# Splitting the expert matrices inside the last attention batch

## The reference

```python
x = x + attention(layernorm(x))          # 16 heads of 32, window of 128 and 4 sink columns
x = x + experts(layernorm(x), token_ids) # below
x = x + ffn(layernorm(x))                # 8-bit activations, ternary weights, hidden 2048
...
tid = clip(token_ids, 0, VOCAB - 1)
expert_ids = minimum(tid // (VOCAB // 4), 3)
for e in range(4):                       # Wg = Wu = Wd = ctx, 4 x 512 x 512
    g = silu(h @ Wg[e].T); u = h @ Wu[e].T
    y = (g * u) @ Wd[e].T
    out = where(expert_ids == e, y, out)
```

## Time and profile before

| | us |
|---|---|
| median of 3 runs | 949.4 (948.38 to 952.41) |
| the profiled execution | 942.91 |
| its span, first to last instruction | 941.4 |
| TensorE busy, whole span | 839.4 (89%) |
| VectorE, ScalarE, GpSimd busy | 628.5, 517.8, 265.0 |
| attention ends, experts begin | about 560.6 |
| experts end, last stage begins | about 713 |

### The profile page before, as it was taken

The page is one execution under the profiler, slowest core; times in us unless marked ns, Lnnn a source line. Parts: engine busy times, 40 slices in busy tenths (PEclk is TensorE's granted clock), DMA queues, the critical chain, the costliest instruction groups (busy, mean ns, idle before and its releaser), DMA issues. The chain is left out here.

```text
span 941.4 us, 17497 instructions
## 1 busy us (share of the span) xinstructions
PE 839.4 (89%) x6031; PEld 545.4 (58%) x6054; DVE 628.5 (67%) x1122; ACT 517.8 (55%) x1136; POOL 265.0 (28%) x258
## 2 busy tenths in 40 slices
PE   4897999979999979999998864999993899999996
PEld 3664666656666756666765543888871344444443
DVE  6655754646655446656456637788863999999994
ACT  4254665545665435666466622544432777777775
POOL 1061301110310011211013124454422444444442
PEclk9998999999999979999999996999997999999998
DMA  7345421462442173344083018446202011110100
GB/s 246 69 106 142 112 72 51 105 143 105 113 113 64 50 180 101 79 113 113 23 234 81 2 53 324 155 152 218 93 37 89 3 44 45 45 45 33 34 34 34
DMA packets 36740, 90.68 MB, mean 96 GB/s; under 512 B 6846, under 2 KB 6846, under 8 KB 35008
## 3 DMA queue, kind: packets, MB, share of 16 engines
q1 hardware_dynamic: 31216, 73.97, 28.0%
q0 software_dynamic: 5456, 15.74, 4.9%
HBM read 52.71 MB, written 13.39 MB: 70 GB/s over the span
## 5 line engine op out<-in xcount | busy, mean ns | idle before, releaser
L457 ACT ACTIVATE probs<-s_ps,neg_max 128x512 f32<-128x512 f32 (+2 forms) x256 | 153.4, 607 | 35.7 <-DVE neg_max L606 34.7
L464 ACT ACTIVATE probsT<-pT_ps 128x512 f32<-128x512 f32 (+1 forms) x128 | 76.2, 596 | 140.1 <-PE pT_ps L815 139.5
L815 PE MATMUL pT_ps<-ident,probs 128*128 128x128 f32 (+1 forms) x960 | 148.0, 283 | 2.5 <-ACT probsT L464 2.5
L606 DVE TENSOR_REDUCE neg_max<-s_ps 128x2 f32<-128x1024 f32 (+2 forms) x128 | 130.6, 1021 | 24.8 <-PE s_ps L796 21.3
L626 DVE COPY probsT<-pT_ps 128x512 f32<-128x512 f32 x112 | 77.4, 691 | 85.5 <-PE pT_ps L815 85.0
L815 PEld LDWEIGHTS pT_ps<-ident,probs 128*128 128x128 f32 (+1 forms) x960 | 101.4, 135 | 35.3 <-issue 23.7
L831 PE MATMUL pv_ps<-probsT,v_sb 128*32 128x128 f32 (+1 forms) x1920 | 102.7, 286 | 11.0 <-DVE probsT L626 9.0
L789 PE MATMUL s_ps<-qk_stack 96*128 96x512 f32 (+2 forms) x256 | 94.8, 438 | 16.0 <-issue 12.1
L1372 POOL TENSOR_TENSOR hw<-h,ln_w_sb 128x512 f32<-128x512 f32 x64 | 81.8, 1278 | 90.3 <-DVE h L1487 90.2
L831 PEld LDWEIGHTS pv_ps<-probsT,v_sb 128*32 128x32 f32 (+1 forms) x1920 | 37.8, 107 | 82.1 <-issue 55.4
L367 POOL TENSOR_TENSOR rinv_wide<-rinv,one_col 128x512 f32<-128x512 f32 x16 | 16.7, 1043 | 227.0 <-DVE rinv L613 227.0
(11 more groups left out here) (236 smaller groups left out, 1804.6 us busy)
## 6 DMA issues: line engine op xcount, KB each, us to landing
qk_stack<-qk_parts SPq DMA_DIRECT2D x192, 128.0 KB, 2.5
w_piece<-w_ffn SPq DMA_DIRECT2D x24, 512.0 KB, 3.7
w_stage<-w_ffn SPq DMA_DIRECT2D x12, 1024.0 KB, 5.1
xres<-x POOLq DMA_DIRECT2D x4, 1024.0 KB, 6.3
xt<-x SPq DMA_DIRECT2D x16, 256.0 KB, 2.6
y<-xt SPq DMA_DIRECT2D x16, 256.0 KB, 2.0
xn<-x SPq DMA_DIRECT2D x3, 1024.0 KB, 11.1
x<-xres POOLq DMA_DIRECT2D x3, 1024.0 KB, 7.7
```

Of the source, the lines that this page charges most:

```text
L457: nc.scalar.activation(probs[:, qt % 2, h, 0:width(qt)], s_ps[:, h, 0:width(qt)], ACT.Exp, bias=neg_max[:, qt % 2, h:h + 1], accum_out=sum ...
L464: nc.scalar.activation(probsT[0:rows, 0, :], pT_ps[0:rows, 0, :], ACT.Identity).then_inc(slot_copied[0], 1)
L606: nc.vector.tensor_reduce(neg_max[:, qt % 2, 2 * s:2 * s + 2], s_ps[:, 2 * s:2 * s + 2, 0:width(qt)], AX.X, ALU.max, negate=True).then_inc ...
L815: last = nc.tensor.transpose(pT_ps[0:z - a, k % 2, h * P:h * P + P], probs[:, qt % 2, h, a:z], ident[:])
```

## The change

- `w_hi` and `w_lo` of the attention become one shared buffer of four places, and the experts' `c_hi` and `c_lo` are the same buffer. Expert `e` overwrites the place of the matrix number `e` of q, k, v, o.
- Experts 0 to 2 are split in the last batch, at the ends of units (2, 0), (2, 2) and (3, 1): `expert_hi` on ScalarE behind the unit's exponentials, `expert_lo` on VectorE behind the unit's last copy. SyncE loads experts 2 and 3 into `xn` and `v_next` when the subtractions of experts 0 and 1 are done. The place of `o` is in use to the end of attention, so expert 3 is split in the expert stage (`last_hi`, `last_lo`).
- `w_piece` is shared, and GpSimd clears it at the end of attention. It holds tiles 0 and 1; `xg_own` has 9 tiles and is cleared at once. The first gather waits for nothing, the second for nothing but the constants before it, the third for the clear.
- On VectorE the last expert's subtraction stands behind `xT_lo` of tile 0; TensorE waits for it ahead of the first product and for no expert after.
- SyncE waits for the second gather instead of the first, and then issues weight chunks only. The last stage's `xt` is `xn`.

```diff
...
 RING = 4
-OWN_TILES = ROUTED_TILES - 2 * TT
+FIRST_TILES = 2
+OWN_TILES = ROUTED_TILES - 2 * TT - FIRST_TILES
 GATHERS_AHEAD = 6
-CLEARED_AT_ONCE = 2
-CLEARS = 3
 ROUTE_COUNTED, ROUTE_STEPS = 10, 32
...
         xn, v_next = sh["xn"], sh["v_next"]
 
-        w_hi = {n: sb(f"w{n}_hi", [P, DK, D], F32R) for n in "qkvo"}
-        w_lo = {n: sb(f"w{n}_lo", [P, DK, D], F32R) for n in "qkvo"}
+        w_hi = {n: sh["w_hi"][:, i * DK:i * DK + DK, :] for i, n in enumerate("qkvo")}
+        w_lo = {n: sh["w_lo"][:, i * DK:i * DK + DK, :] for i, n in enumerate("qkvo")}
...
 
         abs_sum = sh["abs_sum"]
-        w_piece = sb("w_piece", [P, CHUNK // 2])
...
         rstd_ready, xn_ready = sem("rstd_ready"), sem("xn_ready")
         side_done, side_hi, side_left = sem("side_done"), sem("side_hi"), sem("side_left")
-        v_moved, experts_loaded = sem("v_moved"), sem("experts_loaded")
-        piece_loaded, piece_done = sem("piece_loaded"), sem("piece_done")
+        v_moved = sem("v_moved")
+        c_loaded = [sem(f"c_loaded{e}") for e in range(EXPERTS)]
+        c_hi_ready, c_lo_ready = sem("c_hi_ready"), sem("c_lo_ready")
...
             return lambda qt: [s if s and s[0] in mine else None for s in sides_of(g, qt)]
 
         STACK_INC = 16 * 3 * GH
...
                         .then_inc(piece_loaded, 16)
 
+                def load_expert(e):
+                    sp.dma_start((xn, v_next)[e % 2][:], io["c"][e].rearrange("(k p) n -> p k n", p=P)).then_inc(c_loaded[e], 16)
...
                         sp.wait_ge(v_moved, BATCH - 1)
-                        for e, buffer in enumerate((xn, v_next)):
-                            sp.dma_start(buffer[:], io["c"][e].rearrange("(k p) n -> p k n", p=P)).then_inc(experts_loaded, 16)
+                        for e in range(2):
+                            load_expert(e)
 
                         sp.wait_ge(scores_ready, units_before(b, 1, TT) * 2)
                         stack(b, 3, nth(b, "K3"))
+                        for e in range(2, EXPERTS):
+                            sp.wait_ge(c_lo_ready, e - 1)
+                            load_expert(e)
 
                 sp.wait_ge(side_left, nth(-1, "K2"))
...
-                sp.wait_ge(experts_loaded, 32)
+                for e in range(EXPERTS):
+                    sp.wait_ge(c_loaded[e], 16)
 
...
                 batch(BATCH - 1, True)
+                pool.wait_ge(piece_done, (BATCH - 1) * PIECES)
+                nc.gpsimd.memset(sh["w_piece"][:], 0.0).then_inc(piece_cleared, 1)
 
             @block.scalar
...
+                    if last and (g, qt) in SPLIT_AT:
+                        expert_hi(SPLIT_AT.index((g, qt)))
                     if g and not last and qt >= TT - 2:
...
+                def expert_hi(e):
+                    act.wait_ge(c_loaded[e], 16)
+                    if e < 2:
+                        act.wait_ge(side_done, nth(BATCH - 1, "QK"[e] + "3"))
+                    nc.scalar.activation(sh["w_hi"][:, e * DK:e * DK + DK, :], (xn, v_next)[e % 2][:], ACT.Identity).then_inc(c_hi_ready, 1)
 
...
+                    if last and (g, qt) in SPLIT_AT:
+                        expert_lo(SPLIT_AT.index((g, qt)))
                     if prepare and qt in (1, 2):
...
                             normalize(b + 1, t)
+
+                def expert_lo(e):
+                    dve.wait_ge(c_hi_ready, e + 1)
+                    at = slice(e * DK, e * DK + DK)
+                    nc.vector.tensor_tensor(sh["w_lo"][:, at, :], (xn, v_next)[e % 2][:], sh["w_hi"][:, at, :].bitcast(F32),
+                                            ALU.subtract).then_inc(c_lo_ready, 1)
 
...
         ident, rows, expert_of = sh["ident"], sh["rows"], sh["expert_of"]
 
-        c_hi = sb("c_hi", [P, EXPERTS * DK, D], F32R)
-        c_lo = sb("c_lo", [P, EXPERTS * DK, D], F32R)
+        c_hi, c_lo = sh["w_hi"], sh["w_lo"]
 
...
         abs_sum, abs_row, w_scale = sh["abs_sum"], sb("abs_row", [P, 3]), sb("w_scale", [P, 3])
         plus_round = sb("plus_round", [P, 1])
         e_ones = sb("e_ones", [P, P])
 
         xg_own = sb("xg_own", [P, OWN_TILES, D])
+        first_homes = [sh["w_piece"][:, t * D:t * D + D] for t in range(FIRST_TILES)]
         late_homes = [sh["xn"][:, t, :] for t in range(TT)] + [sh["v_next"][:, t, :] for t in range(TT)]
-        xg = [xg_own[:, s, :] for s in range(OWN_TILES)] + late_homes
+        xg = first_homes + [xg_own[:, s, :] for s in range(OWN_TILES)] + late_homes
         assert len(xg) == ROUTED_TILES
         bn_st, bn_mv = sb("e_bn_st", [P, 2, 6]), sb("e_bn_mv", [P, 2, 2])
...
-        c_loaded = {e: sem(f"c_loaded{e}") for e in range(2, EXPERTS)}
         consts, rows_cleared = sem("e_consts"), sem("rows_cleared")
-        c_hi_ready, c_lo_ready = sem("c_hi_ready"), sem("c_lo_ready")
+        last_hi_ready, last_lo_ready = sem("last_hi_ready"), sem("last_lo_ready")
...
-            return (n + 2) % STAGES
+            return n % STAGES
...
 
-                sp.wait_ge(gathered[0], 16)
-                for e in range(2, EXPERTS):
-                    sp.dma_start(c_stage[e], io["c"][e].rearrange("(k p) n -> p k n", p=P)).then_inc(c_loaded[e], 16)
+                sp.wait_ge(gathered[1], 16)
                 for n in range(CHUNKS):
-                    if n in (2, 3):
-                        sp.wait_ge(c_lo_ready, (n + 1) * DK)
-                    elif n >= STAGES:
+                    if n >= STAGES:
                         sp.wait_ge(w_clipped, n - STAGES + 1)
                     sp.dma_start(w_stage[:, stage_of(n), :], io["w_ffn"][n]).then_inc(w_loaded[stage_of(n)], 16)
...
+
+                def gather(s):
+                    if FIRST_TILES <= s < FIRST_TILES + OWN_TILES:
+                        pool.wait_ge(rows_cleared, 1)
+                    elif s == FIRST_TILES + OWN_TILES + TT:
+                        pool.wait_ge(last_lo_ready, 1)
+                    nc.gpsimd.indirect_dma_start(xg[s], None, x1, bass.IndirectOffsetOnAxis(rows[:, s:s + 1], 0),
...
-                        pool.wait_ge(rows_cleared, min(s // CLEARED_AT_ONCE, CLEARS - 1) + 1)
-                    else:
-                        pool.wait_ge(c_lo_ready, ((s - OWN_TILES) // TT + 1) * DK)
-                    nc.gpsimd.indirect_dma_start(xg[s], None, x1, bass.IndirectOffsetOnAxis(rows[:, s:s + 1], 0),
...
-                    pool.wait_ge(x2_ready, s + 1)
-                    nc.gpsimd.indirect_dma_start(x2, bass.IndirectOffsetOnAxis(rows[:, s:s + 1], 0), xg[s], None,
-                                                 bounds_check=last_row, oob_is_err=False).then_inc(scattered, 16)
-
-                def rstd_of(s):
-                    h = s % 2
-                    pool.wait_ge(eps_added, s + 1)
-                    nc.gpsimd.tensor_tensor(rstd[:, h:h + 1], var_eps[:, h:h + 1], minus_half[:], ALU.pow).then_inc(rstd_ready, 1)
-
-                last_row = nc.gpsimd.to_reg(TOK - 1)
...
-                    if e >= 2:
-                        act.wait_ge(c_loaded[e], 16)
-                    nc.scalar.activation(c_hi[:, e * DK:e * DK + DK, :], c_stage[e], ACT.Identity).then_inc(c_hi_ready, 1)
+                def last_hi():
+                    at = slice((EXPERTS - 1) * DK, EXPERTS * DK)
+                    nc.scalar.activation(c_hi[:, at, :], sh["v_next"][:], ACT.Identity).then_inc(last_hi_ready, 1)
...
                         .then_inc(w_shifted, 1)
 
+                last_hi()
                 act.wait_ge(consts, 3)
-                for e in range(2):
-                    expert_hi(e)
                 xT_hi_of(0)
-                for e in range(2, EXPERTS):
-                    expert_hi(e)
...
             @block.vector
             def _(dve):
-                def expert_lo(e):
-                    dve.wait_ge(c_hi_ready, e + 1)
-                    nc.vector.tensor_tensor(c_lo[:, e * DK:e * DK + DK, :], c_stage[e],
-                                            c_hi[:, e * DK:e * DK + DK, :].bitcast(F32), ALU.subtract).then_inc(c_lo_ready, DK)
-
+                def last_lo():
+                    at = slice((EXPERTS - 1) * DK, EXPERTS * DK)
+                    dve.wait_ge(last_hi_ready, 1)
...
 
-                for m in range(CLEARS - 1):
-                    nc.vector.memset(xg_own[:, m * CLEARED_AT_ONCE:(m + 1) * CLEARED_AT_ONCE, :], 0.0).then_inc(rows_cleared, 1)
-                dve.wait_ge(consts, 3)
-
+                nc.vector.memset(xg_own[:], 0.0).then_inc(rows_cleared, 1)
                 nc.vector.tensor_reduce(abs_row[:], abs_sum[:].rearrange("p n w -> p w n"), AX.X, ALU.add).then_inc(row_summed, 1)
 
-                expert_lo(0)
                 for s in range(2):
                     stats_of(s)
                     dve.wait_ge(stats_step, s + 1)
                     variance_of(s)
                     normalize(s)
                 xT_lo_of(0)
-                nc.vector.memset(xg_own[:, (CLEARS - 1) * CLEARED_AT_ONCE:, :], 0.0).then_inc(rows_cleared, 1)
-                for e in range(1, EXPERTS):
```

(45 more changed lines are left out.)

10 lines of the change are left out of this document (4 added, 6 removed).

## The result

| | kernel before | changed | ratio, 95% interval |
|---|---|---|---|
| first comparison, median us | 949.55 | 961.79 | 1.0096 (1.006 to 1.0131) |
| second comparison, median us | 955.85 | 959.88 | 1.006 (1.0029 to 1.009) |

The change makes the kernel slower, by 0.6% to 1.0% in its two comparisons, and both intervals lie above 1. The first rests on four runs of each kernel, the second on 31 and 10. The ratios are not the quotients of the medians, which are 1.0129 and 1.0042. I had forecast 950.7 us, a range of 945.5 to 956, and no difference.

The account below looks back on a forecast made before the run. TensorE was taken to bound attention and later expert tiles, VectorE's order the expert stage's start. Splits +6.5 and start -5.2 gave +1.3 us: 944.2 profiled, 950.7 as median, range 945.5 to 956.

Parts of the forecast that it names:

- What bounds it: TensorE bounds late attention and the later expert tiles; at the expert stage's start VectorE's order makes TensorE wait 6.21 us.
- my 5.2: Start of the expert stage: gain from earlier gathers and multiply and from tile 1's product at full clock, 5.2 us.
- The first gather wasn't blocked: Expert-stage start: a rival had the long clear hold the first gather, everything behind 3.2 us later, 953.9; chance 0.10.
- the third took 1.0 us: Third gather at the expert stage's start: taken as 1.05 us with no subtraction beside it, 2.23 as the bound.
- The new wait on the last subtraction: Expert-stage start: TensorE's first product waits for the last expert's subtraction and starts 1.3 us later, near 573.0.
- The walk through the three splits: Last attention batch: VectorE's subtractions wait for ScalarE and delay maximum and copy, TensorE late by 6.5 us in all.
- The rival that they are hidden: Last attention batch: VectorE's idle pieces absorb the splits, attention costs 0 and the kernel takes 944.2 us; chance 0.10.
- That they pass in full: Last attention batch: the three pairs cost their whole 12.4 us, net +7.2, 956.6 us; chance 0.10.
- the 9 at which I had said I would be wrong: Sign at attention's end: the prediction is wrong if that end moves by less than 3 or more than 9 us.
- one earlier pause of 1.97 us: TensorE's pause at 45.96, which left the clock up; cited against a clock fall, while one of 6.21 brought it down.
- That rival, "One of them gives about 954, two give 957": TensorE's pauses in attention drop its clock, some 3 us each, or tile 1 stays slow, 2 to 3; chance 0.10.
- the 6.5 us between profile and median: Whole kernel: the median of 949.4 lies 6.5 us above the profiled 942.9; the same difference turned 944.2 into 950.7.

Follow-up runs that it names:

- the three with the short one: Against the changed kernel: splits in halves or later subtractions, four tiles cleared first, the other five behind tile 0's low part; ratios to before 0.9925, 0.9951, 1.0011 (scatters also moved).
- the half that it stretched to 3.27 us: Changed kernel with each split cut into two halves of 1024 columns, VectorE's halves one unit behind ScalarE's; 948.44 us, ratio to before 0.9931.

## Why the prediction was wrong

**What bounds it, and what was gained.** This held. The start of the expert stage gained 6.2 us and gave 0.7 back in the exit, 5.5 against my 5.2. The first gather wasn't blocked and the third took 1.0 us, as I had it from the shorter row. The new wait on the last subtraction cost 0.9 us counted from the first clear, where I had 1.3. Counted from the end of attention it cost 1.7: VectorE's first clear came 0.7 us later after the last additions in the changed kernel and in all variants with the long clear, and 0.2 later in the three with the short one, while ScalarE's table load, its first instruction of the stage, came at the same 5.3 us in all. GpSimd's first gather came 6.1 us after the last additions in all of them, 0.8 behind where its first instruction had stood and where I had put the gather. I can't say why.

**The walk through the three splits.** It gave 2.15 + 2.65 + 1.7 = 6.5. With the clock held up the attention lost 6.04 (4.25 in the first two, 1.8 in the third). So the walk was near in size and named the right queue. It did not have GpSimd's addition beside the first split, which by the half that it stretched to 3.27 us would have held the subtraction there even without the wait for ScalarE. Moved to later units the subtractions cost 0.2, so the delay is one of place and order and not of the work. The rival that they are hidden was wrong for this placement. That they pass in full was wrong too: its 12.4 lies within the 11.4 to 14.2 measured, but only by luck, since the delays made 6.04 of it.

**The failed step is the clock.** The attention's end moved by 11.4 and 14.2 us, beyond the 9 at which I had said I would be wrong. I put the pauses at 1.7 to 2.4 us, they measured 1.5 to 2.0, and took from one earlier pause of 1.97 us that the clock survives them; I gave the fall 0.10 and left it out of the sum. It fell in both profiles, twice each, for 17 and 31 us of time, and cost 5.4 and 8.2 us, about as much as the delays themselves. My price of some 3 us for a fall was near for three of the four (1.9, 3.4 and 3.3 us) and short for the one that lasted 20.5 us (4.9). One row of a survived pause was no bound: one and the same pause (1.91 us, first split) brought the clock down in one execution and not in the other. The Trainium skill, TensorE: Matmul & The Clock Gate, section What's actually happening, has the clock set by how busy TensorE has recently been, and this case agrees with it: filling the pauses alone kept it at 1.00. I had cited the page for the variation of a start and not applied it to a fall. That rival, "One of them gives about 954, two give 957", is the case that came, with 6.04 + 5.4 to 8.2 - 5.5 = +5.9 to +8.7 us, 955 to 958 on the first median.

**The median.** I carried the 6.5 us between profile and median through as a constant. No run bears that out. The kernel before had medians of 949.55 to 955.85 in its sets, and its second profile lay 5.8 over its median instead of 6.5 under. The stall that the first profile lacked is part of this; how the rest comes about is open. It leaves the forecast difference alone but not the absolute time: the measured 961.8, a median of four runs, lies 4 to 6 above what the traces' difference and the first median give, and no run explains that.

## What to carry to other kernels

An operation of two engines in series should be queued with the second part a step behind the first: the same three subtractions cost 6 us directly behind their producer and 0.2 a unit or two later, order and place together. Look at the third engine as well: beside GpSimd's addition half a subtraction took 3.27 us instead of 1.22. When a change makes TensorE pause again and again in a stretch that was busy before, price a fall of the clock as a term of the sum: it doubled the cost here, and the same pause brought it in one execution and not in the other. And take a second profile of the kernel before, before a profile's distance to the median is used.

## What the runs showed of the hardware that I had not expected

The clock fell at pauses of 1.5 to 2.0 us in a stretch where TensorE worked 41.4 of 47.0 us before, and one such fall lasted 20.5 us. What ends such a fall was not tried. While sixteen scatters of 128 words run, some 0.96 us of GpSimd each, or just behind them, VectorE or ScalarE stood still for 8.6 to 15.2 us at a time in eleven of twelve profiles, also in the one where the scatters were moved; the twelfth had none of it. A subtraction of VectorE (1024 columns, both inputs in SBUF) took 3.27 us beside an addition of GpSimd and 1.22 without one. A gather that GpSimd began beside a subtraction of 2048 columns took 1.9 to 2.8 us, the others 1.0 to 1.2, one wholly beside a clear 1.03.
